# Attention with split fp32 products: value products of the next pair inside a pair, output products inside the next

## The reference, cut to what matters

```python
# x: (2, 1024, 256), 16 heads of 128, after a layer norm
q = einsum('bpd,hde->bphe', x, W_Q) + b_Q      # k and v likewise
scores = einsum('bqhe,bkhe->bhqk', q, k) / sqrt(128)
scores = where(causal, scores, -100000.0)
attn = softmax(scores, axis=-1)
z = einsum('bkhe,bhqk->bqhe', v, attn)
out = einsum('bqhe,hed->bqd', z, W_O) + b_O
```

## Time and profile before

| | |
|---|---|
| median of 3 runs | 2081.06 us (2079.89 to 2084.43) |
| the profiled execution, its own time | 2083.12 us |
| its span in the profile | 2081.4 us |
| TensorE busy in the span | 1857.4 us, 89% |
| VectorE, ScalarE, GpSimd busy | 1360.8, 978.3, 650.6 us |
| granted TensorE clock, mean | 0.95 |

### The profile page before, as it was taken

The page is one execution under the profiler, slowest core; times in us unless marked ns, Lnnn a source line. Parts: engine busy times, 40 slices in busy tenths (PEclk is TensorE's granted clock), DMA queues, the critical chain, the costliest instruction groups (busy, mean ns, idle before and its releaser), DMA issues.

```text
span 2081.4 us, 33572 instructions
## 1 busy us (share of the span) xinstructions
PE 1857.4 (89%) x10614; PEld 1534.3 (74%) x10614; DVE 1360.8 (65%) x2745; ACT 978.3 (47%) x1984; POOL 650.6 (31%) x644
## 2 busy tenths in 40 slices
PE   2699889878899999999999979999999986999997
PEld 1455555567778778888888868888888874788776
DVE  6655463278865666666666656666666674788887
ACT  2333233245533466566566546665656652233332
POOL 5123233433433332222232223222222221343342
PEclk9789879889999999999999999999999997899998
DMA  3000001010010100000000000000000001000001
GB/s 97 1 1 1 1 0 41 1 61 16 6 19 1 22 21 20 20 20 0 20 20 5 16 21 22 20 20 20 19 1 20 5 0 46 16 16 30 15 0 41
DMA packets 59807, 37.71 MB, mean 18 GB/s; under 512 B 16488, under 2 KB 56656, under 8 KB 59728
## 3 DMA queue, kind: packets, MB, share of 16 engines
q1 hardware_dynamic: 59728, 36.71, 6.2%
HBM read 34.60 MB, written 2.10 MB: 18 GB/s over the span
## 4 chain that ended last, share of the span: by engine, by line
PE 71%; DVE 15%; ACT 5%; issue 4%; DVEq 3%; POOL 1%; ACTq 0%; DMA 0%; POOLq 0%
PE psum L52 12%; PE psum L53 12%; PE psum L54 12%; PE psum L1580 6%; PE psum L1570 3%; PE psum L1593 3%; PE psum L1572 3%; PE psum L1571 3%; PE psum L1594 3%; PE psum L1601 3%; DVE mamba_conv_sum L1093 3%; PE psum L971 2%; PE psum L969 2%; DVE table_leaves L579 2%; PE psum L960 1%
## 5 line engine op out<-in xcount | busy, mean ns | idle before, releaser
L1732 POOL TENSOR_SCALAR attn_probs<-attn_probs,attn_inverse 128x128 f32<-128x128 f32 (+7 forms) x256 | 191.2, 747 | 577.9 <-DVE attn_inverse L1696 577.2
L1641 ACT ACTIVATE attn_pt_hi<-psum 128x512 fp32r<-128x512 f32 (+3 forms) x384 | 184.1, 485 | 215.7 <-PE psum L1580 213.5
L1688 DVE TENSOR_TENSOR attn_pt_lo<-psum,attn_pt_hi 128x512 fp32r<-128x512 f32 (+3 forms) x384 | 210.6, 553 | 67.1 <-ACT attn_pt_hi L1641 64.9
L1646 ACT ACTIVATE attn_probs<-attn_probs,attn_neg_max 128x128 f32<-128x128 f32 (+7 forms) x256 | 197.9, 773 | 99.5 <-DVE attn_neg_max L1692 99.2
L1580 PE MATMUL psum<-ident,attn_probs 128*128 128x128 f32 x1152 | 190.2, 277 | 33.9 <-DVE attn_pt_lo L1688 18.7
L1692 DVE CUSTOM_DVE_ANT_0 attn_probs<-psum,attn_mask 128x128 f32<-128x128 f32 (+7 forms) x256 | 192.7, 753 | 16.4 <-PE psum L1572 8.8
L1593 PE MATMUL psum<-attn_pt_hi,attn_v_hi 128*128 128x512 f32 (+3 forms) x384 | 161.1, 420 | 26.1 <-DVE attn_pt_lo L1688 19.4
L1580 PEld LDWEIGHTS psum<-ident,attn_probs 128*128 128x128 f32 x1152 | 137.8, 142 | 55.7 <-DVE attn_pt_lo L1688 24.8
L2008 POOL TENSOR_TENSOR moe_hid_lo<-moe_hidden,moe_hid_hi 128x512 fp32r<-128x512 f32 x64 | 82.9, 1296 | 197.9 <-ACT moe_hid_hi L1981 197.9
L1570 PE MATMUL psum<-attn_k_hi,attn_q_hi 128*128 128x512 f32 (+3 forms) x384 | 133.9, 349 | 2.6 <-DVE attn_neg_max L1692 2.5
L1594 PE MATMUL psum<-attn_pt_lo,attn_v_hi 128*128 128x512 f32 (+3 forms) x384 | 133.8, 348 | 0.0
(11 more groups left out here) (321 smaller groups left out, 5377.9 us busy)
## 6 DMA issues: line engine op xcount, KB each, us to landing
attn_qkv_raw<-in_L_attn_W_Q_dram SPq DMA_DIRECT2D x32, 128.0 KB, 2.2
attn_qkv_raw<-in_L_attn_W_K_dram SPq DMA_DIRECT2D x32, 128.0 KB, 2.4
attn_qkv_raw<-in_L_attn_W_V_dram SPq DMA_DIRECT2D x32, 128.0 KB, 2.6
attn_wo_raw<-in_L_attn_W_O_dram SPq DMA_DIRECT2D x16, 256.0 KB, 3.1
moe_gu_raw<-_L_ffn_gate_up_proj_dram SPq DMA_DIRECT2D x8, 512.0 KB, 3.8
x_in<-_attn_hidden_states_dram SPq DMA_DIRECT2D x4, 512.0 KB, 5.6
x_tok<-_attn_hidden_states_dram SPq DMA_DIRECT2D x4, 512.0 KB, 5.9
moe_down_raw<-in_L_ffn_down_proj_dram SPq DMA_DIRECT2D x8, 256.0 KB, 4.4
```

The lines of the kernel that those rows point to most:

```text
L1646: act.activation(probs_view(e), probs_view(e), ACT.Exp, bias=stat(neg_max, e), scale=-1.0, accum_out=stat(sums, e)).then_inc(exp_done, 1)
L1688: dve.tensor_tensor(lo, work_view(e), hi.bitcast(F32), ALU.subtract).then_inc(work_done, 1)
```

## The change

It takes the four `values` and four `output` events out of the end of the pair. The value products of the next pair go behind positions 17, 19, 21 and 23, each behind the exp of its position. The output products of a pair go into the next pair, behind positions 0, 1, 4 and 5. So that the first pair of a batch has no outputs of a pair before it, a new list "start" is written out for it, and the loop runs 6 times instead of 7. The last pair does its own first two outputs behind positions 18 and 20 and the other two at its end. The split of the output weights moves from position 3 (1 in the last pair) to 7 and waits there for the outputs that still read the old ones. The waits for `z` and for weights in `output` follow. The number of matmuls, copies and adds doesn't change.

```diff
--- before.py
+++ after.py
@@ -1319,9 +1319,11 @@
             return [lambda m=m, half=half: add("project", ("work", "hi"), m=m, h=h, half=half)
                     for m in (Q, K) for half in range(HALF)]
 
-        def values():
-            for t in range(QT // 2):
-                add("values", ("work", "hi"), t=t)
+        def values(t):
+            add("values", ("work", "hi"), t=t)
+
+        def output(t, z):
+            add("output", ("work",), t=t, need_z=z)
 
         def score(h, t, need):
             return add("score", ("tile",), h=h, t=t, need=need)
@@ -1329,12 +1331,13 @@
         if kind == "first":
             n["qkv"] += 1
             for m in (Q, K, V):
-                add("split", ("w",), m=m)
+                add("split", ("w",), m=m, free=0)
             for h in range(2):
                 for p in project(h):
                     p()
             need = n["work"]
-            values()
+            for t in range(QT // 2):
+                values(t)
             late = None
             for t in range(QT):
                 e = score(0, t, need)
@@ -1351,7 +1354,10 @@
             score_at = {0: 0, 2: 1, 3: 2, 5: 3, 6: 4, 8: 5, 9: 6, 11: 7}
             project_at = (3, 6, 8, 10)
             norm_at = {0: ("stats", 0), 2: ("apply", 0), 4: ("turn", 0), 6: ("stats", 1), 8: ("apply", 1), 10: ("turn", 1)}
-            splits = {1: 3} if last else {0: Q, 1: K, 2: V, 3: 3}
+            splits = {7: 3} if last else {0: Q, 1: K, 2: V, 7: 3}
+            before_outputs = {} if kind == "start" else {0: 0, 1: 1, 4: 2, 5: 3}
+            own_outputs = {18: 0, 20: 1} if last else {}
+            values_at = {} if last else {17: 0, 19: 1, 21: 2, 23: 3}
             turned, late, need = [], None, 0
 
             def turn(c):
@@ -1369,7 +1375,7 @@
 
                     e = score(1 - h, score_at[c % half], need)
                 if c in splits:
-                    add("split", ("w",), m=splits[c])
+                    add("split", ("w",), m=splits[c], free=n["work"] if splits[c] == 3 else 0)
                 if c + 2 < len(chunks):
                     turn(c + 2)
                 if last and c - half in norm_at:
@@ -1385,32 +1391,37 @@
                     project(h)[project_at.index(c % half)]()
                     if c == half - 1:
                         need = n["work"]
+                if c in before_outputs:
+                    output(before_outputs[c], 0 if before_outputs[c] >= HALF else -1)
+                if c in own_outputs:
+                    output(own_outputs[c], 3)
+                if c in values_at:
+                    values(values_at[c])
             if late:
                 events.append(dict(late, what="invert"))
-            if not last:
-                values()
-            for t in range(QT // 2):
-                add("output", ("work",), t=t)
+            if last:
+                for t in range(HALF, QT // 2):
+                    output(t, 4)
         return events, n
 
-    sections = {kind: section(kind) for kind in ("first", "body", "last")}
+    sections = {kind: section(kind) for kind in ("first", "start", "body", "last")}
 
     def sections_of(engine, handle):
 
         counts = Counts()
         for b in range(BATCH):
-            for kind in ("first", "body", "last"):
+            for kind in ("first", "start", "body", "last"):
                 events, n = sections[kind]
                 if kind == "body":
-                    with engine.Fori(0, PAIRS - 1) as i:
+                    with engine.Fori(0, PAIRS - 2) as i:
                         counts.i, counts.per = i, n
                         for e in events:
-                            handle(e, counts, b, kind, i)
+                            handle(e, counts, b, kind, i + 1)
                     counts.i = None
-                    counts.passed(n, PAIRS - 1)
+                    counts.passed(n, PAIRS - 2)
                 else:
                     for e in events:
-                        handle(e, counts, b, kind, 0 if kind == "first" else PAIRS - 1)
+                        handle(e, counts, b, kind, PAIRS - 1 if kind == "last" else 0)
                     counts.passed(n)
 
     def norm_group(e, b):
@@ -1514,12 +1525,15 @@
             else:
                 load_qkv(0)
             counts.passed(sections["first"][1])
-            with sp.Fori(0, PAIRS - 1) as i:
+            load_qkv(1)
+            load_wo(0)
+            counts.passed(sections["start"][1])
+            with sp.Fori(0, PAIRS - 2) as i:
                 counts.i, counts.per = i, sections["body"][1]
-                load_qkv(i + 1)
-                load_wo(i)
+                load_qkv(i + 2)
+                load_wo(i + 1)
             counts.i = None
-            counts.passed(sections["body"][1], PAIRS - 1)
+            counts.passed(sections["body"][1], PAIRS - 2)
             load_wo(PAIRS - 1)
             counts.passed(sections["last"][1])
 
@@ -1602,8 +1616,8 @@
                 last.then_inc(summed, 1)
             elif what == "output":
 
-                pe.wait_ge(z_done, 1 + counts.at("z", 4))
-                pe.wait_ge(w_split, counts.at("w", 1 if kind == "last" else 4))
+                pe.wait_ge(z_done, 1 + counts.at("z", e["need_z"]))
+                pe.wait_ge(w_split, counts.at("w", (1 if kind == "last" else 4) if e["need_z"] > 0 else 0))
                 for t in range(2):
                     tokens = slice((2 * e["t"] + t) * P, (2 * e["t"] + t + 1) * P)
                     for h in range(2):
@@ -1627,7 +1641,7 @@
                     act.wait_ge(wo_loaded, 16 * (counts.at("wo", 1)))
                 else:
                     act.wait_ge(qkv_loaded, 16 * QKV_LOADS * (counts.at("qkv", 1)))
-                act.wait_ge(work_ready, counts.at("work", 0))
+                act.wait_ge(work_ready, counts.at("work", e["free"]))
                 act.activation(hi, raw, ACT.Copy).then_inc(w_hi, 1)
             elif what in ("project", "values", "turn"):
                 act.wait_ge(work_ready, counts.at("work", e["work"] + 1))
@@ -1735,7 +1749,7 @@
         sections_of(pool, handle)
 
     n = sections
-    total = BATCH * (n["first"][1]["work"] + (PAIRS - 1) * n["body"][1]["work"] + n["last"][1]["work"])
+    total = BATCH * (n["first"][1]["work"] + n["start"][1]["work"] + (PAIRS - 2) * n["body"][1]["work"] + n["last"][1]["work"])
     return dict(sync=sync, sync_early=sync_early, split_early=split_early, tensor=tensor, scalar=scalar, vector=vector, gpsimd=gpsimd, done=(work_done, total))
```

## The result

The changed kernel takes 2117.28 us (median of 4 runs, 2115.05 to 2123.43) against 2081.14: a ratio of 1.0176, 95% interval 1.0151 to 1.0200. That is 36.1 us slower; 35 was forecast.

The account below looks back on a forecast made before the run. TensorE's order was taken to bound the kernel (busy 1857.4 of 2081.4 us). Boundary wait 23.9 plus clock 14 minus last pairs 3 makes 35 us slower, 2116 us against the median 2081.1; range 2099 to 2129.

Parts of the forecast that it names:

- The wait at the boundary: Between pairs, last value products to turn 0 takes 4.14 us instead of 12.42; 1.71 us more per boundary, 23.9 for 14.
- (b): Wait of a pair's first sum for the low part of its transposed probabilities, 0.72 us; claimed to stay.
- (c): Wait of the second head's first sum for bank 7 to be read, 0.37 us; claimed to stay.
- (d): Transpose's wait for the chain from position 11's score through GpSimd's scaling, 1.33 us; claimed to stay.
- positions 0 to 5 or 17 to 23: Where the moved products go; TensorE hardly waits there, and new waits there would show the prediction wrong.
- The clock: TensorE's clock falls to 1.2 GHz at most boundaries: 1.0 us each, 14 us in all, bounds 0 and 24.
- the sum was 45: Whole change by the skill's rule, clock falling every turn: 23.9 + 24 - 3 = 45 us slower.
- The last pairs: Last pair of each batch, two outputs moved ahead of holes in TensorE's work: 3 us gained for both batches.
- The clock held: Rival: the clock doesn't fall at the boundaries, 21 us slower, 2102 us; chance 0.20.
- ScalarE not held up: Rival: last high part of values isn't behind the exp, turn 0 comes 1.1 us earlier, 2086 us; chance 0.06.
- Faster: Rival: spreading the events evens VectorE's and ScalarE's load, (b), (c) and (d) vanish, 2068 us; chance 0.06.

Follow-up runs that it names:

- run 1: Changed kernel with the fourth value products put ahead of the gather and exp at position 23, on every queue: 2107.5 us.
- run 6: Changed kernel with outputs 0 and 1 back at the pair's own end behind the fourth value products, outputs 2 and 3 in the next pair: 2076.94 us.
- run 3: Changed kernel with only the value products moved inside the pair, the four outputs at its end as in the kernel before: 2098.46 us.
- run 4: Changed kernel with only two value products moved inside (behind positions 17 and 19), the other two and all four outputs at the end: 2082.57 us.
- Runs 7 and 8: Kernel before, fourth output after next pair's turn 0, banks rotating over the boundary: 2056.47 us; then also two projections moved behind positions 11 and 13: 2036.32 us.
- run 2: Changed kernel with 18 matmuls that nobody reads added ahead of turn 0, 14 times: 2099.38 us.
- run 5: Changed kernel with only the outputs moved into the next pair, the four value products staying at the end: 2092.2 us.

## Why the prediction was right

**The wait at the boundary.** 4.14 us from the last value products to turn 0 were forecast and 4.14 measured; 63.4 us for a pair with the clock up, and 63.48. The chain gather, exp, high part, low part could be read from the trace of before because it was all there, hidden. That it hangs on ScalarE's queue order only in part is shown by run 1, and that cover behind the last value products is what hides it by run 6.

**(b), (c), (d).** (b) kept its 0.72 us where the clock was up (0.72 at 793.82). (c) went from 0.37 to 0.46 and (d) from 1.33 to 1.28, so (d) did shrink, by 0.05, and the two together went from 1.70 to 1.74. No wait appeared at positions 0 to 5 or 17 to 23 of a loop pair. Runs 3 and 4 show that the places the value products were sent to had nothing to fill. Runs 7 and 8 are the counterpart: products sent to where the waits are gain most of them.

**The clock.** Priced at 1.0 us a boundary, with bounds 0 and 1.7. The six pairs from the first boundary last 388.27 us in the changed kernel and 380.77 in run 2, so 7.5/6 = 1.25 us a boundary (389.05 against 380.77 in the second batch, 1.38), and run 2 is 17.9 us faster in all. The mechanism was right; the term of 14 us should have been about 18. A single stretch of 3.4 us costs 0.7 to 0.8 us, less than the price, because part of it falls on wait (b), as the prediction said: at 855.07 turn 0 takes 1.23 us and sum 0 behind it doesn't wait. The term was undersized because in four of the twelve loop pairs the clock stays down for 6.8 us, which costs 2.6 (66.04 - 63.48 = 2.56) and lies above the bound of 1.7 for one boundary. At a boundary the trace before showed no such stretch, but in the last pair of the second batch it did (0.57 is the granted clock from 1716 to 1728), so a wider bound could have been read from it.

By the rule quoted from the Trainium skill ("TensorE: Matmul & The Clock Gate", section "HAM oscillation — how this bites in real kernels"), a fall in every turn of the loop, the sum was 45. The trace agrees with the fall in eleven of the twelve loop pairs and in both last pairs; the measured 36 is less than 45 because the falls cost about 18 us and not 24, and because the last pairs gained more.

**The last pairs.** A gain of 3 us was taken, bounds 0 and 5.8. From the last turn 0 of a batch to the first matmul of the next stage before took 53.29 and 52.69 us. It takes 57.52 and 55.01 now, with four output products of 5.76 us more in it: gains of 1.5 and 3.4, 5 us. The clock's fall behind the last boundary of each batch is already taken off in them. In run 2, which hasn't these two falls, it takes 56.68 and 52.30 us, gains of 2.4 and 6.2.

The spans of the two profiled executions are 34.7 us apart (2116.10 - 2081.40). They are made of 14 x 1.75 = 24.5 for the wait, 15.8 for the clock in the twelve loop pairs, 1.1 in the first pairs of the two batches, -5 for the last pairs, 0.2 ahead of the attention and -1.9 in the stage behind it (last section). The medians are 36.1 apart. So the wait's term held; the clock cost 15.8 in the loop pairs where 12 x 1.0 was priced; the last pairs came to -5 where -3 and two boundaries at 1.0 make -1; and the other three pieces weren't thought of. These errors cancel, so that 2116 came within 1.3 us is partly luck.

**The rivals.** The clock held: refuted by the window at 0.53 and run 2. ScalarE not held up: refuted by 790.15, directly behind the exp. Faster: refuted by the unchanged waits and run 4.

**What stays open.** Why the clock stays down for one stretch in some pairs, for two in others and in one pair doesn't fall, with the same instructions and the same wait of 2.52 us, wasn't tried.

## What to carry to other kernels

Before moving work out of a stretch, write down every chain that the stretch hides: here it hid the values' way through ScalarE and VectorE behind gather and exp, and the chain through `z` as well, and run 3 cost 17 us for the second. Send moved work to where the busiest engine waits, which the timeline names to the microsecond, and not to where the other engines are merely less loaded. A wait with "everything before is done" at a loop's edge is worth replacing by the one that its buffer needs, with one piece of work between the producer and its first reader.

## What was not expected of the hardware

TensorE matmuls whose result nobody reads made the changed kernel 17.9 us faster, because the clock stayed at 2.4 GHz behind them (granted clock 1.00 in all twelve loop pairs). The fall can come after less standing still than the 2.5 us of this change: with waits of 1.5 and 0.7 us (run 5) it comes in six of twelve loop pairs. With 0.86 and 0.72 us (run 4) it comes in one of twelve, where the granted clock is 0.50 from 1102.30 to 1105.70, and in the kernel before, with the same two waits, in none. So that a clock stayed up at a wait in one profiled execution doesn't show that it always will. The same code behind the attention took 348.4 us before and 346.5 in the changed kernel, at a mean clock of 0.92 in both:

```profile
1732.99:2081.40 348.41, 310.49 (x1640) 260.77 (x1640) 274.92 (x451) 104.91 (x173) 120.05 (x90) 0.92 0.08 25
```

```profile
1769.58:2116.10 346.52, 308.63 (x1640) 259.17 (x1640) 274.84 (x451) 104.81 (x173) 120.17 (x90) 0.92 0.08 25
```

So a microsecond or two between two kernels can come from a stage that neither changes; over the ten kernels here that stage took between 346.0 and 349.6 us.
